# Division in the mixing stage of a decoder layer: logarithm, exponential and a Newton step in place of a reciprocal

## The chip, the cores and the metric

The kernel runs on one core of a Trainium2 chip. The metric is the device time of one execution, in microseconds (us), as the median of several runs. Engines are named as the profile names them: PE is TensorE, DVE is VectorE, ACT is ScalarE, POOL is GpSimd, SP issues DMAs.

## The reference, cut to what matters

The layer is an RWKV mixing, a cross attention, and a causal attention with a mixture of experts, each with a residual and a layer norm, on 16 x 128 tokens of 256 channels. Only the mixing is touched. For every channel it runs this scan over the 128 tokens of each batch, once forward and once backward:

```
ku = k_t + u
m = jnp.maximum(mx, ku)
e1 = jnp.exp(mx - m)
e2 = jnp.exp(ku - m)
y = (e1 * num + e2 * v_t) / (e1 * den + e2)
...
out_f = jax.nn.sigmoid(r_f) * wkv(k_f, v_f, -jnp.exp(time_decay), time_first, False)
```

The sigmoid's denominator, 1 + exp(-r), and the scan's denominator are multiplied together, so that there is one division for each element of the result: y = num / ((1 + exp(-r)) * den).

## The kernel before, in words

Seven stages run one after the other: preparing weights, mixing, cross attention, attention, routing, experts, finish. Each engine has its own instruction stream, written out by hand in program order, and semaphores tie the streams together. There is no scheduler: what stands behind a waiting instruction on its engine waits too.

The mixing cuts the work into 4 groups (`g`) of 4 batches = 512 token columns, and each group into 4 units (`u`): direction x half of the channels. So there are 16 units, n = 0 to 15, each on tiles of 128 channels x 512 tokens in f32. `in_groups` writes the first and the last group out and loops over the two between. For unit n:

- PE projects r, k and v into three PSUM banks (L519).
- ACT, `begin`: exp(-r) into `gate` (L565), v out of PSUM into `values` (L567), then, when DVE's `gaps` are there, two Relu and one Exp over `weight` (L570, L572, L574).
- DVE, `gaps`: the running maximum of the keys (L642, four scans that read PSUM) and two differences (L650, L652, one operand in PSUM).
- POOL, `new_parts`: two products of 128x512 (L596, L598). DVE, `scans`: two scans of 128x512 over SBUF tiles (L658, L661), for denominator and numerator. POOL, `add_old`: two products and two sums of 128x512 (L607 twice, L610, L611), which leave the denominator in `sums[p][:, 1]` and the numerator in `sums[p][:, 0]`.
- DVE, `finish`: (gate + 1) * denominator (L668), its reciprocal (L671), times the numerator into `y` (L675).
- PE adds y's projection to rows in PSUM (L534). At u = 2 DVE takes the previous group's layer norm statistics from them (`norm`, L681 to L689), POOL raises them to the power -1/2 (L615), and at u = 3 DVE scales the rows (`norm_rows`, L695).

The streams are staggered. In DVE's step n stand scans(n), gaps(n+2), at u = 3 norm_rows, then finish(n-1), and at u = 2 norm. In ACT's step n stands begin(n+2). In POOL's step n stand new_parts(n+1) and add_old(n). `gate` and `weight` have a buffer for each of the 4 units, `sums`, `values`, `new_value`, `carry` and `top` two each.

Of the kernel before, what the change touches and what calls it, by code (L numbers as in the profile page):

```python
# [32 lines left out]
UNITS = 4  # L33
# [14 lines left out]
BANKS_JOB = 4  # L48
MAGIC = 12582912.0
LOWEST = -1e38  # L50
MASKED = -1e30
EPS = 1e-5

# [42 lines left out]
class Shared:  # L96


    def __init__(self, nc, t, out, top):
# [17 lines left out]
        self.magic = self.buffer(top, "magic", [1])  # L117
        self.minus_magic = self.buffer(top, "minus_magic", [1])
        self.minus_half = self.buffer(top, "minus_half", [4])
        self.logits = self.buffer(top, "logits", [B, E])  # L120
        self.ident16 = self.buffer(top, "ident16", [P], BF16)
        self.shares = self.buffer(top, "shares", [2, B])
# [48 lines left out]
    def begin(self, sp, stage):  # L171

        sp.sem_inc(self.begun, 1)
# [249 lines left out]
def mix_stage(k):  # L423
# [31 lines left out]
    scans_ready = k.semaphore("scans_ready")  # L455
    sums_ready = k.semaphore("sums_ready")
    unit_done = k.semaphore("unit_done")
    unit_joined = k.semaphore("unit_joined")
    mix_var = k.semaphore("mix_var")
    mix_scale = k.semaphore("mix_scale")  # L460
# [96 lines left out]
    def scalar(act):  # L557
        st = k.steps["act"]

        def begin(u, n):  # L560

            p = u % 2
            act.wait_ge(rkv_ready, n + 1)
            act.wait_ge(unit_done, n + 1)
            act.activation(gate[u][:, :], banks[:, 3 * p, :], ACT.Exp, scale=-1.0)  # L565
            act.wait_ge(new_ready, 2 * n + 2)
            act.copy(values[p][:, :], banks[:, 3 * p + 2, :]).then_inc(vr_ready, 1)  # L567
            act.wait_ge(gaps_ready, n + 1)
            w = weight[u]
            st.did(act.activation(w[:, INNER, :], w[:, EDGES, :], ACT.Relu))  # L570
            st.wait()
            st.did(act.activation(w[:, EDGES, :], w[:, EDGES, :], ACT.Relu, scale=-1.0))  # L572
            st.wait()
            act.activation(w[:, :, :], w[:, :, :], ACT.Exp, scale=-1.0).then_inc(weights_ready, 1)  # L574

        def step(u, n, g, is_first, is_last):
            if u < 2 or not is_last:
                begin((u + 2) % UNITS, n + 2)

        act.wait_ge(k.begun, k.begins["mix"])  # L580
        act.wait_ge(k.mix_loads, 16 * LOADS)
        act.activation(step_decay[:, :], decay[:, :], ACT.Exp).then_inc(decay_ready, 1)
        begin(0, 0)
        begin(1, 1)
        st.done(1, 4)
        in_groups(step, act, st, 2 * UNITS)
        st.done(1, st.at)

    def gpsimd(pool):
# [43 lines left out]
    def vector(dve):  # L633
# [21 lines left out]
        def scans(u, n):  # L655
# [5 lines left out]
            dve.tensor_tensor_scan(carry[p][:, 0, 1:GT + 1], weight[u][:, FROM_PAST, :], new_value[p][:, 0, :],  # L661
                                   0.0, ALU.mult, ALU.add).then_inc(scans_ready, 1)

        def finish(u, n):

            p = u % 2
            dve.wait_ge(sums_ready, n + 5)
            st.did(dve.scalar_tensor_tensor(out=gate[u][:, :], in0=gate[u][:, :], scalar=1.0, in1=sums[p][:, 1, :],  # L668
                                            op0=ALU.add, op1=ALU.mult))
            st.wait()  # L670
            st.did(dve.reciprocal(sums[p][:, 1, :], gate[u][:, :]))  # L671
            st.wait()
            num, rec = (sums[p][:, m, :].rearrange("p (b s) -> p b s", b=GB) for m in range(2))
            to = y[:, u, :, :] if u < DC else y[:, u, :, ::-1]
            dve.tensor_tensor(to, num, rec, ALU.mult).then_inc(unit_done, 1)  # L675

        def norm(g):
            dve.wait_ge(unit_joined, UNITS * g + UNITS)
# [19 lines left out]

        def step(u, n, g, is_first, is_last):
            scans(u, n)  # L700
            if u < 2 or not is_last:
                gaps((u + 2) % UNITS, n + 2)
            if u == 3 and not is_first:
                norm_rows(g - 1)
            if u and not is_first:
                dve.wait_ge(unit_joined, n - UNITS)
            if u or not is_first:
                finish((u - 1) % UNITS, n - 1)
            if u == 2 and not is_first:
                norm(g - 1)  # L710
# [13 lines left out]
        gaps(1, 1)  # L724
        st.done(1, st.at)
        in_groups(step, dve, st, 3 * UNITS + 2)
        finish(UNITS - 1, N - 1)
        norm(GROUPS - 1)
        norm_rows(GROUPS - 1)
# [1522 lines left out]
def decoder_layer(nc, t, out):  # L2252
    with ExitStack() as top:
# [18 lines left out]
        @block.vector  # L2272
        def _(dve):
            k.steps["dve"] = Steps(dve, steps["dve"])
            dve.memset(k.magic[:, :], MAGIC).then_inc(k.s_fill, 1)
            dve.memset(k.minus_magic[:, :], -MAGIC).then_inc(k.s_fill, 1)
            dve.memset(k.minus_half[:, :], -0.5).then_inc(k.s_fill, 1)
            dve.wait_ge(k.s_consts, 16)
            for _, _, vector, *_ in stages:
                vector(dve)  # L2280

        @block.scalar
        def _(act):
            k.steps["act"] = Steps(act, steps["act"])
            act.wait_ge(k.s_consts, 16)
            act.wait_ge(k.s_fill, 3)
            for _, _, _, scalar, _ in stages:
                scalar(act)

        @block.gpsimd  # L2290
        def _(pool):
            k.steps["pool"] = Steps(pool, steps["pool"])
            pool.wait_ge(k.s_consts, 16)
            pool.wait_ge(k.s_fill, 3)
            for _, _, _, _, gpsimd in stages:
                gpsimd(pool)

# [75 lines left out]
```

## Time and profile before

| | |
|---|---|
| median of 3 runs | 1294.68 us (1290.55 to 1294.69) |
| the profiled execution's own time | 1292.86 us |
| its span in the trace | 1291.1 us |
| busy over the whole span | PE 78%, DVE 78%, ACT 57%, POOL 47% |
| mixing stage in the trace | from about 128 to 332 us |
| ACT_TABLE_LOAD | 2 in the whole kernel |

The shares are means over seven stages with different limits. The mixing stage is about a sixth of the span, and its own shares are in the rows further down.

### The profile page before, as it was taken

To read this page: it belongs to the slowest core of one execution; us is meant where nothing else is said; L and a number is where in the kernel's file an instruction comes from. 1 tells how busy PE (TensorE), PEld (TensorE's weight loads), DVE (VectorE), ACT (ScalarE), POOL (GpSimd) and SP (SyncE) were. 2 spreads that over 40 slices of the span, in tenths; PEclk is the share of its full clock that TensorE was granted. 3 is DMA by queue.
4 is the path that set the end of the run, shared out by engine and by line. 5 is a ranking of instruction groups with operands and counts; after the bars stand their busy time and mean duration, and the time that the engine had idled before them with its cause. 6 is when DMAs were issued, how large, how long until landed. Compare 5 with 4: busy or idle time off the path is not lost.

```text
span 1291.1 us, 25737 instructions
## 1 busy us (share of the span) xinstructions
PE 1005.1 (78%) x7366; PEld 756.9 (59%) x7367; DVE 1004.6 (78%) x2283; ACT 738.8 (57%) x1866; POOL 608.9 (47%) x805
## 2 busy tenths in 40 slices
PE   0334886772588898896799999983799999999980
PEld 0233332341477776774467767653688888888870
DVE  6894899999789888983788888856577777767755
ACT  4785644341488888882465555540566666666650
POOL 3896787776244444441255555543232332332225
PEclk9666978985789888986899999996899999999995
DMA  4953200002233333322123222230111111111105
GB/s 182 399 199 117 92 1 22 11 32 76 84 112 110 110 110 110 110 75 65 33 69 103 85 85 85 82 112 7 36 36 37 41 35 37 41 36 35 41 28 195
DMA packets 51884, 105.70 MB, mean 82 GB/s; under 512 B 9808, under 2 KB 36432, under 8 KB 51328
## 3 DMA queue, kind: packets, MB, share of 16 engines
q1 hardware_dynamic: 47472, 92.39, 20.8%
q0 software_dynamic: 4368, 12.78, 3.2%
q8 instruction: 20, 0.33, 0.1%
q14 instruction: 24, 0.20, 0.0%
HBM read 73.06 MB, written 32.10 MB: 81 GB/s over the span
## 4 chain that ended last, share of the span: by engine, by line
PE 48%; DVE 21%; issue 10%; POOL 6%; ACT 4%; DMA 1%; DVEq 0%; POOLq 0%; SPq 0%; ACTq 0%
PE banks L1996 14%; PE banks L2006 10%; PE banks L1360 4%; PE banks L1403 4%; DVE mix_sums L671 4%; PE banks L1382 2%; PE banks L1395 2%; POOL whole L1119 2%; PE banks L1352 2%; DVE carry L661 2%; ACT whole_level L1047 2%; DVE carry L658 2%; DVE whole_stat L227 2%; DVE peak L1150 1%; DVE top L642 1%
## 5 line engine op out<-in xcount | busy, mean ns | idle before, releaser
L2079 DVE SCALAR_TENSOR_TENSOR expert_gate<-banks,expert_steps,expert_chunk 128x128 f32<-128x128 f32 x546 | 166.1, 346 | 97.1 <-ACT expert_chunk L2041 92.7
L1996 PE MATMUL banks<-expert_parts,levels 128*128 128x128 bf16 x3276 | 228.8, 220 | 8.5 <-issue 5.6
L1996 PEld LDWEIGHTS banks<-expert_parts,levels 128*128 x3276 | 202.7, 98 | 49.2 <-issue 21.5
L2006 PE MATMUL banks<-down,up 128*128 x546 | 176.1, 406 | 0.0
L2041 ACT COPY expert_chunk<-banks 128x256 f32<-128x256 f32 x273 | 101.7, 372 | 102.4 <-PE banks L1996 87.9
L2134 POOL DMA_INDIRECT chosen_d<-expert_y,expert_target x39 | 39.1, 1001 | 203.5 <-ACT expert_y L2051 203.5
L519 PE MATMUL banks<-x_turned,w_rkv 128*128 128x512 f32 (+1 forms) x192 | 98.1, 670 | 38.8 <-DVE weight L652 38.3
L2045 ACT ACTIVATE silu<-expert_gate,expert_steps 128x128 f32<-128x128 f32 x273 | 110.7, 405 | 16.9 <-DVE expert_gate L2079 16.7
L414 PE MATMUL banks<-consts,level 128*128 128x128 f32 x154 | 35.6, 423 | 87.8 <-POOL level L397 87.8
L1119 POOL TENSOR_TENSOR whole<-whole_level,whole_stat 128x896 bf16<-128x896 f32 x32 | 53.3, 1686 | 102.4 <-DVE whole_level L1188 102.4
L2086 DVE SCALAR_TENSOR_TENSOR up<-expert_gate,expert_steps,silu 128x128 f32<-128x128 f32 x273 | 94.0, 344 | 9.3 <-ACT silu L2045 9.3
L519 PEld LDWEIGHTS banks<-x_turned,w_rkv 128*128 128x128 f32 x192 | 40.5, 217 | 94.1 <-issue 93.1
L1047 ACT ACTIVATE whole_level<-whole_raw,whole_stat 128x128 f32<-128x128 f32 x224 | 91.2, 485 | 6.9 <-DVE whole_stat L244 6.9
L414 PEld LDWEIGHTS banks<-consts,level 128*128 128x128 f32 x154 | 31.3, 226 | 91.3 <-POOL level L397 44.0
L2006 PEld LDWEIGHTS banks<-down,up 128*128 128x128 f32 x546 | 83.0, 191 | 0.4
L364 ACT ACTIVATE level<-raw,magic,stat 128x128 f32<-128x128 f32 x154 | 60.3, 480 | 20.0 <-DVE stat L263 20.0
L942 PE MATMUL banks<-v_ones,probs_t 128*128 128x17 f32 x512 | 63.7, 267 | 0.0
L1575 POOL TENSOR_TENSOR att_probs<-att_probs,att_share 128x1024 f32<-128x1024 f32 x16 | 30.4, 1897 | 70.2 <-DVE att_share L1692 70.2
L942 PEld LDWEIGHTS banks<-v_ones,probs_t 128*128 128x128 f32 x512 | 62.3, 199 | 0.0
L920 PE MATMUL banks<-spread,q_t 64*128 64x512 f32 x128 | 44.1, 768 | 23.2 <-DVE probs L1153 22.3
L1360 PE MATMUL banks<-attend_w,xn_t 128*128 128x512 f32 x128 | 59.0, 604 | 0.0
L1403 PE MATMUL banks<-attend_w,o_turn 128*128 128x256 f32 x256 | 58.1, 380 | 0.5 <-ACT logits L1506 0.5
(237 smaller groups left out, 2512.7 us busy)
## 6 DMA issues: line engine op xcount, KB each, us to landing
whole_raw<-in_weight_jobs SPq DMA_DIRECT2D x16, 896.0 KB, 5.3
raw<-in_weight_jobs SPq DMA_DIRECT2D x11, 896.0 KB, 5.4
numbers_d<-turned SPq DMA_DIRECT2D x11, 896.0 KB, 5.0
levels_d<-whole_t SPq DMA_DIRECT2D x16, 448.0 KB, 2.7
levels<-levels_d SPq DMA_DIRECT2D x16, 448.0 KB, 3.8
down<-numbers_d SPq DMA_DIRECT2D x16, 448.0 KB, 4.4
finish_moe<-chosen_d SPq DMA_DIRECT2D x8, 512.0 KB, 7.5
normed_d<-normed_parts SPq DMA_DIRECT2D x16, 192.0 KB, 1.9
```

The source lines that it names most:

```text
L519: last = pe.matmul(banks[:, 3 * (u % 2) + m, :], w_rkv[:, kc, col:col + P], x_turned[d][:, kc, bass.ds(g * GT, GT)], start=(kc == 0), stop ...
L942: last = pe.matmul(banks[:, HEADS, head * (XK + 1):(head + 1) * (XK + 1)], probs_t[h][:, 4 * m + a, :], v_ones[j][:, head, :], start=True, ...
L1047: last = act.activation(level[j][:, a, :], raw[j][:, a, :], ACT.Identity, bias=stat[j][:, BIAS, a:a + 1], scale=stat[j][:, INV, a:a + 1])
L1119: last = pool.tensor_tensor(whole[j][:, half, :], level[j][:, half, :], wide(stat[j][:, BIAS, half], P), ALU.subtract)
L1360: last = pe.matmul(banks[:, Q + m, :], xn_t[:, c, :], w_qkv[:, c, 512 * m:512 * m + 512], start=(c == 0), stop=(c == DC - 1))
L1403: last = pe.matmul(banks[:, TURN, 0:D], o_turn[:, h, :], w_o[:, h, :], start=(h == 0), stop=(h == QH - 1))
L1996: last = pe.matmul(banks[:, at, (m * DC + c) * ROWS:(m * DC + c + 1) * ROWS], levels[:, bass.ds(expert * (2 * JOB) + (m * JOB + (f * DC + ...
L2006: last = pe.matmul(banks[:, Y + j, 0:D], up[j][:, f, :], down[:, bass.ds(expert * JOB + f * D, D)], start=(f == 0), stop=(f == FC - 1))
L2041: act.copy(chunk[slot(j, f)][:, :, :], halves(at)[:, :, 0, :]).then_inc(chunk_ready, 1)
L2045: act.activation(silu[slot(j, f)][:, :], gate[slot(j, f)][:, 0, :], ACT.Silu, scale=steps[j][:, 0, 0, f:f + 1]).then_inc(silu_ready, 1)
L2079: last = dve.scalar_tensor_tensor(out=gate[slot(j, f)][:, m, :], in0=halves(at)[:, m, 1, :], scalar=steps[j][:, m, 1, f:f + 1], in1=chunk[ ...
L2086: dve.scalar_tensor_tensor(out=up[j][:, f, :], in0=gate[slot(j, f)][:, 1, :], scalar=steps[j][:, 1, 0, f:f + 1], in1=silu[slot(j, f)][:, : ...
```

## The change

`finish` is cut in two. DVE's `product(n-1)` multiplies gate and denominator; it now stands right behind scans(n), ahead of gaps(n+2), and waits for POOL's sums of unit n-1 and for `gates_ready`. The 1 + is taken out of it: ACT adds the one in `begin` (an Identity with a bias tile `ones`), and the product caps the gate at 1e30 instead. ACT's new `invert(n-1)` takes the logarithm of the product and then exp(-that). DVE's `finish(n-1)`, where it stood, makes one Newton step of two operations and the product with the numerator. ACT's former `begin` is split, so that its step is begin(n+2), invert(n-1), weigh(n+2). Three semaphores and one 128x1 buffer are new, with its fill at the kernel's start.

```diff
             act.wait_ge(unit_done, n + 1)
-            act.activation(gate[u][:, :], banks[:, 3 * p, :], ACT.Exp, scale=-1.0)
+            st.did(act.activation(gate[u][:, :], banks[:, 3 * p, :], ACT.Exp, scale=-1.0))
             act.wait_ge(new_ready, 2 * n + 2)
             act.copy(values[p][:, :], banks[:, 3 * p + 2, :]).then_inc(vr_ready, 1)
+            st.wait()
+            act.activation(gate[u][:, :], gate[u][:, :], ACT.Identity, bias=k.ones[:, 0:1]).then_inc(gates_ready, 1)
+
+        def weigh(u, n):
+
             act.wait_ge(gaps_ready, n + 1)
...
+        def invert(u, n):
+
+            p = u % 2
+            act.wait_ge(product_ready, n + 1)
+            st.did(act.activation(sums[p][:, 1, :], gate[u][:, :], ACT.Ln))
+            st.wait()
+            act.activation(sums[p][:, 1, :], sums[p][:, 1, :], ACT.Exp, scale=-1.0).then_inc(inverse_ready, 1)
+
         def step(u, n, g, is_first, is_last):
             if u < 2 or not is_last:
                 begin((u + 2) % UNITS, n + 2)
+            if u or not is_first:
+                invert((u - 1) % UNITS, n - 1)
+            if u < 2 or not is_last:
+                weigh((u + 2) % UNITS, n + 2)
...
-        def finish(u, n):
+        def product(u, n):
 
             p = u % 2
             dve.wait_ge(sums_ready, n + 5)
-            st.did(dve.scalar_tensor_tensor(out=gate[u][:, :], in0=gate[u][:, :], scalar=1.0, in1=sums[p][:, 1, :],
-                                            op0=ALU.add, op1=ALU.mult))
-            st.wait()
-            st.did(dve.reciprocal(sums[p][:, 1, :], gate[u][:, :]))
+            dve.wait_ge(gates_ready, n + 1)
+            dve.scalar_tensor_tensor(out=gate[u][:, :], in0=gate[u][:, :], scalar=LARGEST, in1=sums[p][:, 1, :],
+                                     op0=ALU.min, op1=ALU.mult).then_inc(product_ready, 1)
+
+        def finish(u, n):
+
+            p = u % 2
+            dve.wait_ge(inverse_ready, n + 1)
+            st.did(dve.tensor_tensor(gate[u][:, :], gate[u][:, :], sums[p][:, 1, :], ALU.mult))
+            st.wait()
+            st.did(dve.scalar_tensor_tensor(out=sums[p][:, 1, :], in0=gate[u][:, :], scalar=2.0, in1=sums[p][:, 1, :],
+                                            op0=ALU.subtract, op1=ALU.mult))
             st.wait()
             num, rec = (sums[p][:, m, :].rearrange("p (b s) -> p b s", b=GB) for m in range(2))
             to = y[:, u, :, :] if u < DC else y[:, u, :, ::-1]
-            dve.tensor_tensor(to, num, rec, ALU.mult).then_inc(unit_done, 1)
+            dve.scalar_tensor_tensor(out=to, in0=num, scalar=-1.0, in1=rec, op0=ALU.mult, op1=ALU.mult).then_inc(unit_done, 1)
...
             scans(u, n)
+            if u or not is_first:
+                product((u - 1) % UNITS, n - 1)
             if u < 2 or not is_last:
                 gaps((u + 2) % UNITS, n + 2)
```

DVE's stream in the kernel before, one step of the mixing loop (u = 1). In these listings the program's scans read as SCALAR_TENSOR_TENSOR with `carry` (`scans`) or `top` (`gaps`) as output.

```order
L658 SCALAR_TENSOR_TENSOR carry<-weight 128x512 [waits weights_ready]
L660 ISA
L661 SCALAR_TENSOR_TENSOR carry<-weight,new_value 128x512 [waits new_ready]
L642 SCALAR_TENSOR_TENSOR top<-step_decay,banks 128x128 [waits rkv_ready]
L642 SCALAR_TENSOR_TENSOR top<-step_decay,banks 128x128 x3
L72 REGISTER_ALU
L650 SCALAR_TENSOR_TENSOR weight<-top,step_decay,banks 128x512 [waits sums_ready,dve_steps]
L652 SCALAR_TENSOR_TENSOR weight<-banks,first,top 128x512
...
L668 SCALAR_TENSOR_TENSOR gate<-gate,mix_sums 128x512 [waits sums_ready]
L72 REGISTER_ALU
L671 RECIPROCAL mix_sums<-gate 128x512 [waits dve_steps]
L72 REGISTER_ALU
L675 TENSOR_TENSOR y<-mix_sums 128x512 [waits dve_steps]
```

The same step of the changed kernel:

```order
L682 SCALAR_TENSOR_TENSOR carry<-weight 128x512 [waits weights_ready]
L684 ISA
L685 SCALAR_TENSOR_TENSOR carry<-weight,new_value 128x512 [waits new_ready]
...
L693 SCALAR_TENSOR_TENSOR gate<-gate,mix_sums 128x512 [waits gates_ready,sums_ready]
L666 SCALAR_TENSOR_TENSOR top<-step_decay,banks 128x128 [waits rkv_ready]
...
L674 SCALAR_TENSOR_TENSOR weight<-top,step_decay,banks 128x512 [waits sums_ready,dve_steps]
L676 SCALAR_TENSOR_TENSOR weight<-banks,first,top 128x512
...
L700 TENSOR_TENSOR gate<-gate,mix_sums 128x512 [waits inverse_ready,unit_joined]
...
L702 SCALAR_TENSOR_TENSOR mix_sums<-gate,mix_sums 128x512 [waits dve_steps]
...
L707 SCALAR_TENSOR_TENSOR y<-mix_sums 128x512 [waits dve_steps]
```

The product of gate and denominator moved from behind the gaps to ahead of them, the reciprocal is gone, and two more operations on SBUF tiles stand in its place.

ACT's stream in the kernel before, one step of the first group:

```order
L565 ACTIVATE gate<-banks 128x512 [waits unit_done,rkv_ready]
L567 COPY values<-banks 128x512 [waits new_ready]
L570 ACTIVATE weight<-weight 128x1024 [waits gaps_ready]
L572 ACTIVATE weight<-weight 128x2x512 [waits act_steps]
L574 ACTIVATE weight<-weight 128x2048 [waits act_steps]
```

The same step of the changed kernel:

```order
L570 ACTIVATE gate<-banks 128x512 [waits unit_done,rkv_ready]
L572 COPY values<-banks 128x512 [waits new_ready]
L574 ACTIVATE gate<-gate,ones 128x512 [waits act_steps]
L590 ACT_TABLE_LOAD
L590 ACTIVATE mix_sums<-gate 128x512 [waits product_ready]
L592 ACT_TABLE_LOAD
L592 ACTIVATE mix_sums<-mix_sums 128x512 [waits act_steps]
L580 ACTIVATE weight<-weight 128x1024 [waits gaps_ready]
L582 ACTIVATE weight<-weight 128x2x512 [waits act_steps]
L584 ACTIVATE weight<-weight 128x2048 [waits act_steps]
```

The Identity, the logarithm and the exponential are new, and the build puts a table load ahead of each of the last two, in every step; the first load stands ahead of the wait for the product, the second behind the logarithm.

## Rows read from the trace of the kernel before

**Rows 1.** Busy time by stretch: the mixing stage; us, then PE, PEld, DVE, ACT, POOL, clock

```profile
128.00:332.00 204.00, 132.36 (x327) 67.36 (x326) 193.77 (x228) 81.23 (x80) 146.48 (x100) 0.84 0.12 42
```

**Rows 2.** Timeline, DVE, step of unit 9; start us, us, engine, line

```profile
239.15 0.69 DVE L675 TENSOR_TENSOR y<-mix_sums 128x512 f32<-128x512 f32 x1
239.75 2.29 DVE L658 TENSOR_TENSOR_SCAN carry<-weight 128x512 f32<-128x512 f32 x1
241.97 2.22 DVE L661 TENSOR_TENSOR_SCAN carry<-weight,new_value 128x512 f32<-128x512 f32 x1
244.11 1.32 DVE L642 TENSOR_TENSOR_SCAN top<-step_decay,banks 128x128 f32<-128x128 f32 x4
...
246.80 0.68 DVE L668 SCALAR_TENSOR_TENSOR gate<-gate,mix_sums 128x512 f32<-128x512 f32 x1
247.51 3.35 DVE L671 RECIPROCAL mix_sums<-gate 128x512 f32<-128x512 f32 x1
250.90 0.69 DVE L675 TENSOR_TENSOR y<-mix_sums 128x512 f32<-128x512 f32 x1
251.51 2.29 DVE L658 TENSOR_TENSOR_SCAN carry<-weight 128x512 f32<-128x512 f32 x1
```

**Rows 3.** Timeline, POOL, the same step

```profile
239.41 1.56 POOL L596 TENSOR_TENSOR new_value<-weight,values 128x512 f32<-128x512 f32 x1 [1.31 <-ACT weight L574]
240.93 2.18 POOL L598 TENSOR_TENSOR new_value<-weight,values 128x512 f32<-128x512 f32 x1
244.40 2.31 POOL L607 TENSOR_TENSOR mix_sums<-weight,carry 128x512 f32<-128x512 f32 x2 [1.29 <-DVE carry L661]
246.79 1.82 POOL L610 TENSOR_TENSOR mix_sums<-mix_sums,weight 128x512 f32<-128x512 f32 x1
248.57 1.27 POOL L611 TENSOR_TENSOR mix_sums<-mix_sums,new_value 128x512 f32<-128x512 f32 x1
```

**Rows 4.** Timeline, DVE, later steps: units 12 and 13, 14, 15, end of the stage

```profile
277.00 2.29 DVE L658 TENSOR_TENSOR_SCAN carry<-weight 128x512 f32<-128x512 f32 x1
...
287.72 2.29 DVE L658 TENSOR_TENSOR_SCAN carry<-weight 128x512 f32<-128x512 f32 x1
...
299.47 2.28 DVE L658 TENSOR_TENSOR_SCAN carry<-weight 128x512 f32<-128x512 f32 x1
...
310.57 1.22 DVE L658 TENSOR_TENSOR_SCAN carry<-weight 128x512 f32<-128x512 f32 x1
311.70 1.20 DVE L661 TENSOR_TENSOR_SCAN carry<-weight,new_value 128x512 f32<-128x512 f32 x1
...
320.00 0.68 DVE L668 SCALAR_TENSOR_TENSOR gate<-gate,mix_sums 128x512 f32<-128x512 f32 x1
...
324.11 0.69 DVE L675 TENSOR_TENSOR y<-mix_sums 128x512 f32<-128x512 f32 x1
```

**Rows 5.** Timeline, DVE, the stage's first steps: units 0, 1 and 4

```profile
150.71 0.69 DVE L668 SCALAR_TENSOR_TENSOR gate<-gate,mix_sums 128x512 f32<-128x512 f32 x1 [0.81 <-POOL mix_sums L611]
...
162.32 1.64 DVE L668 SCALAR_TENSOR_TENSOR gate<-gate,mix_sums 128x512 f32<-128x512 f32 x1
...
181.13 2.28 DVE L658 TENSOR_TENSOR_SCAN carry<-weight 128x512 f32<-128x512 f32 x1
```

**Rows 6.** Timeline, ACT, the step of rows 2

```profile
239.93 0.60 ACT L565 ACTIVATE gate<-banks 128x512 f32<-128x512 f32 x1 [0.68 <-DVE y L675]
240.42 0.58 ACT L567 COPY values<-banks 128x512 f32<-128x512 f32 x1
246.91 1.06 ACT L570 ACTIVATE weight<-weight 128x1024 f32<-128x1024 f32 x1 [5.91 <-DVE weight L652]
...
249.09 1.91 ACT L574 ACTIVATE weight<-weight 128x2048 f32<-128x2048 f32 x1
```

**Rows 7.** Timeline, ACT, the table load in the experts stage

```profile
913.40 0.37 ACT L2041 COPY expert_chunk<-banks 128x256 f32<-128x256 f32 x1 [0.85 <-PE banks L1996]
913.79 1.28 ACT L2045 ACT_TABLE_LOAD   x1
915.08 0.40 ACT L2045 ACTIVATE silu<-expert_gate,expert_steps 128x128 f32<-128x128 f32 x1
```

More of the change, by code:

```diff
@@ L50 @@
 LOWEST = -1e38
+LARGEST = 1e30
 MASKED = -1e30
@@ L119, in __init__ @@
         self.minus_half = self.buffer(top, "minus_half", [4])
+        self.ones = self.buffer(top, "ones", [1])
         self.logits = self.buffer(top, "logits", [B, E])
@@ L457, in mix_stage @@
     unit_done = k.semaphore("unit_done")
+    product_ready = k.semaphore("product_ready")
+    inverse_ready = k.semaphore("inverse_ready")
+    gates_ready = k.semaphore("gates_ready")
     unit_joined = k.semaphore("unit_joined")
@@ L582, in scalar @@
         act.activation(step_decay[:, :], decay[:, :], ACT.Exp).then_inc(decay_ready, 1)
[L583 to L586, printed above, removed]
+        for n in range(2):
+            begin(n, n)
+            weigh(n, n)
+        st.done(1, st.at)
+        in_groups(step, act, st, 4 * UNITS)
+        invert(UNITS - 1, N - 1)
         st.done(1, st.at)
@@ L662, in scans @@
                                    0.0, ALU.mult, ALU.add).then_inc(scans_ready, 1)
+        def product(u, n):
+            p = u % 2
+            dve.wait_ge(sums_ready, n + 5)
+            dve.wait_ge(gates_ready, n + 1)
+            dve.scalar_tensor_tensor(out=gate[u][:, :], in0=gate[u][:, :], scalar=LARGEST, in1=sums[p][:, 1, :],
+                                     op0=ALU.min, op1=ALU.mult).then_inc(product_ready, 1)
         def finish(u, n):
             p = u % 2
-            dve.wait_ge(sums_ready, n + 5)
-            st.did(dve.scalar_tensor_tensor(out=gate[u][:, :], in0=gate[u][:, :], scalar=1.0, in1=sums[p][:, 1, :],
-                                            op0=ALU.add, op1=ALU.mult))
+            dve.wait_ge(inverse_ready, n + 1)
+            st.did(dve.tensor_tensor(gate[u][:, :], gate[u][:, :], sums[p][:, 1, :], ALU.mult))
             st.wait()
-            st.did(dve.reciprocal(sums[p][:, 1, :], gate[u][:, :]))
+            st.did(dve.scalar_tensor_tensor(out=sums[p][:, 1, :], in0=gate[u][:, :], scalar=2.0, in1=sums[p][:, 1, :],
+                                            op0=ALU.subtract, op1=ALU.mult))
             st.wait()
@@ L726, in vector @@
         in_groups(step, dve, st, 3 * UNITS + 2)
+        product(UNITS - 1, N - 1)
         finish(UNITS - 1, N - 1)
@@ L2277, in _ @@
             dve.memset(k.minus_half[:, :], -0.5).then_inc(k.s_fill, 1)
+            dve.memset(k.ones[:, :], 1.0).then_inc(k.s_fill, 1)
             dve.wait_ge(k.s_consts, 16)
@@ L2285, in _ @@
             act.wait_ge(k.s_consts, 16)
-            act.wait_ge(k.s_fill, 3)
+            act.wait_ge(k.s_fill, 4)
             for _, _, _, scalar, _ in stages:
@@ L2293, in _ @@
             pool.wait_ge(k.s_consts, 16)
-            pool.wait_ge(k.s_fill, 3)
+            pool.wait_ge(k.s_fill, 4)
             for _, _, _, _, gpsimd in stages:
```

## The prediction

> **What bounds the kernel now.** I read the mixing stage by itself, since nothing else is touched: the busy time by stretch first, then the timelines of DVE, POOL and ACT side by side over one step, then the stage's two ends. In the stage DVE is busy 193.8 of 204 us, POOL 146.5, ACT 81.2 [rows 1]. DVE has no idle time in a steady step: from one L658 to the next is 251.51 - 239.75 = 11.76 us [rows 2], namely scans 4.36 (239.75 to 244.11), gaps 2.69 (to 246.80), L668 0.71, reciprocal 3.39, L675 0.61. The step is as long as DVE's stream. What the reader is to see next is that the scans are not as long as they could be. Where POOL is not at the same work, one follows the other after 1.13 us (310.57 to 311.70) [rows 4]; in the steady step they take 2.2 each, while POOL's L596 and L598, which take 1.27 like L611 when alone, last 1.56 and 2.18 [rows 3]. Laid side by side the four go one after another: L675 ends at 239.84, and from there to 244.11 are 4.27 us for two scans (2 x 1.07) and two POOL operations (2 x 1.07). So a POOL operation and a DVE operation with two SBUF operands exclude each other, and whoever waited goes next. It also holds for short ones: POOL's L610 beside L668 has 1.82 instead of 1.27, 0.55 longer, and L668 itself, 0.68 when alone, has 1.64 where POOL held first [rows 3, 5]. The reciprocal reads one operand and lies beside L610 and L611 at no cost to L611. So the reciprocal's 3.39 us are also a stretch in which POOL has the way free.
>
> The Trainium skill says the same in "SBUF — State Buffer", section on the ports of SBUF: VectorE and GpSimd share a port pair, a VectorE operation with two SBUF inputs takes it, and it is held for the whole instruction while the other blocks. The trace agrees in kind (0.55 us longer); if each were to hold for its full record (1.27 and 0.69 rather than 1.1 and 0.55), the step worked out below would be 12.0 instead of 11.5 us.
>
> **The change, part by part.** DVE, per unit: the reciprocal goes, -3.39. L668 stays as the product, 0.66. Two operations come, each 0.71 with its wait, as L668 to L671 in [rows 2]. Without any contention DVE's step would be scans 2.26, product 0.66, gaps 2.69, three finishing operations 0.71 + 0.71 + 0.61: 7.6 us. With the contention of before on the scans (4.36 instead of 2.26) it is 9.7, 2.0 less than now.
>
> ACT, per unit: exp and copy 1.07 (239.93 to 241.00) and the three on `weight` 4.09 (246.91 to 251.00) stay [rows 6]. New are Identity, Ln and Exp of 128x512, for which I take L565's 0.60 each, and two table loads of 1.28 [rows 7]. Sum 1.07 + 4.09 + 1.8 + 2.56 = 9.5 us. In [rows 7] the load starts 0.02 us behind the end of the copy ahead of it (913.77), and the next activation starts 0.01 behind its end, so a load is 1.3 us here and nothing more. The first load stands ahead of the wait and is hidden in ACT's idle time, the second is in the chain: from the product's end to the inverse there are Ln 0.6, load 1.28, Exp 0.6 and hand-overs, 2.65 us. The gaps behind the product take 2.69 us on DVE, so this is just covered where there are gaps. If that cover is gone (units 13 to 15, no gaps left) it is exposed.
>
> What is late next is the shared way to SBUF. Per step POOL has six operations there and DVE had four (two scans, L668, L675); now DVE has six. In lock time: POOL 6 x 1.1 = 6.6, scans 2.1, and 0.55 for each short one: before 2 x 0.55, sum 9.8; after 4 x 0.55, sum 10.9 of a step of 11.76. I lay a steady step out, from the first scan at 0. The weights for the next unit come at about 0.3, so L596 falls between the scans: scan 1.1, L596 2.2, scan 3.3, L598 4.4, product 4.95, its next instruction 5.07. POOL's two L607 then run beside the gaps, 4.95 to 7.35 with their 2.39 to the next operation (244.40 to 246.79 [rows 3]), L610 to 8.5. Gaps end at 7.76, and the inverse is ready at 7.7, but the first Newton operation waits for L610: 8.5 to 9.05. L611 waited and takes 9.05 to 10.15, the second Newton operation waits for it until 10.7, the last one runs 10.85 to 11.4, next scan 11.45. So the two added short operations cost not 1.4 but 1.4 plus two waits of about 1 us, and the step is **11.5 against 11.76**. ACT's weights are ready at 7.76 + 4.09 = 11.85, that is 0.4 into the next step, which closes the circle; ACT has 2 us to spare.
>
> With norm at u = 2 the step has 2.07 more, as before. At u = 3 POOL is held by L615 until the scans are through, and its L596 then stands against the product: 11.6. At u = 0 the step was 10.72 (277.00 to 287.72 [rows 4]), since POOL's L596 was ahead by then; that advantage goes, because POOL's last operation of the step before is now late: 11.5. A group is 11.5 + 13.5 + 11.6 + 11.5 = 48.1, against 299.47 - 251.51 = 47.96 [rows 2, 4]. From unit 4 to unit 14 that makes +0.9 us; if POOL's operation counts 1.22 rather than 1.1 (L610 and L611 stand 1.78 apart with one L668 between them), the same layout gives 11.9 and +3.1. I take +1.5, nearer the first, since the four that surely exclude each other gave 1.07.
>
> The start: the product now stands ahead of gaps(3) and waits for POOL's first sums, which came at 150.7 with DVE already waiting 0.81 behind the gaps [rows 5]. gaps(3), 2.69 us, now lie behind that wait, and so do the weights of unit 3. Laid out in the same way, unit 4's scan comes at 183.4 instead of 181.13: +2.3 (bounds: 0 if POOL's backlog hides it, 4 for gaps and the inverse exposed once).
>
> The last group: at unit 14 no gaps cover the inverse. Product at 4.95, inverse at 7.7, against L610 and L611, then norm: 13.5 against 310.57 - 299.47 = 11.1: +2.4. Unit 15: norm_rows (1.8) covers part of the inverse and POOL has no L596 and L598: 9.4 against 320.00 - 310.57 = 9.43: 0. The tail: L668 at 320.00 to the end of L675 at 324.80 is 4.8; after it is 0.66 + 2.65 + 0.71 + 0.71 + 0.69 = 5.4: +0.6.
>
> Sum: 2.3 + 1.5 + 2.4 + 0 + 0.6 = **+6.8 us**. The bias tile and its fill at the start lie beside the first loads. ACT's Identity delays the first weights by 0.6, which is in the start's term. PE has 132 of 204 us in the stage and is two units ahead; its clock there is 0.84 of full speed. The stages behind start when the mixed rows are stored, so the stage's end moves theirs one for one. Against the profiled execution (time 1292.86, span 1291.1) this is 1299.7. The median of the runs is 1.8 above the profiled one, so I say 1300.
>
> **Rivals.**
>
> A. The way to SBUF is full and takes back what the reciprocal gives, as above: +2 to +10 us, 1296 to 1304. For it: scans and L596/L598 in a strict row [rows 2, 3]. Against: the order in which the waiting ones go is seen there on long operations only. Chance 0.72.
>
> B. Faster: the short operations slip between POOL's, because POOL waits at its own hand-overs (c. 0.1 us each) and DVE wins. Then the step falls towards DVE's 9.7 or ACT's 9.5. At 9.7 it is 12 steps x 2.0 = -24, plus 5 for both ends: 1274; at 10.9, the lock time alone, 12 x 0.85 = -10, plus 5: 1288. For it: L668 at 246.80 got through although POOL's L610 started at 246.79. It decides from a gain of 0.5 us a step on, where the ends are paid for. Chance 0.16.
>
> C. Slower by far: ACT becomes the bound. It has 9.5 of 11.5 us; from 1 us more for each load on it does. The Trainium skill, "ScalarE: Activation LUTs", section on what a table load costs, gives about 1283 ns and a further drain of about 1380 ns for each switch of set; the row agrees with the first and has nothing of the second. If a load did cost twice its own 1.28, ACT's step would be 9.5 + 2.6 = 12.1 against A's 11.5, and the chain from product to inverse 1.3 longer at three places without cover: 12 x 0.6 + 3 x 1.3 = 11 on top of A's 6.8, 1311. Chance 0.12.
>
> **How the numbers follow.** The likeliest is A at 1300. About 0.5% (6.5 us) is what this kernel's measurement tells from no change: faster is below 1288.2, slower above 1301.2. A puts 0.40 of its chance within and 0.30 above, with 0.02 below; B gives 0.12 faster and 0.04 within; C gives 0.11 slower and 0.01 within. Faster 0.14, same 0.45, slower 0.41. The range 1287 to 1307 holds A, the upper part of B and the lower part of C, and leaves out some 0.2. A's own range is 1296 to 1304.
>
> **What would show it.** In the changed profile: the first Newton operation (L700) and the second (L702) have records of well over 0.7 us, about 1.3 to 1.7, at most units; L707 about 0.7. No reciprocal in the mixing. 32 table loads of 1.28 us, the next activation right behind each. ACT busy about 81 + 16 x 4.4 = 151 us of the stage. POOL's L611-like operation about 1.3 to 1.8. DVE busy about as before, though its work alone is less. Steps of 11.3 to 12 us. DVE's idle time ahead of L700 is small, but for the last three units (2.7 us each at most). The prediction is wrong if L700 and L702 are 0.7 each and the step is under 11 us, or if DVE waits for ACT in steady steps.

## The result and the profile after

The changed kernel takes 1295.47 us (median of 20 runs, 1292.72 to 1298.44), the kernel before 1291.61 us (median of 20, 1286.06 to 1295.42). The ratio is 1.0029, 95% interval 1.0015 to 1.0042: 3.7 us slower by the ratio, and clearly so, though less than 0.5%. The mixing stage, from the first scan to the end of the last `y`, was 187.62 us (137.18 to 324.80) and is 192.10 us (139.02 to 331.12) in the profiled execution of each kernel: +4.5 us.

Timeline of the changed kernel, DVE in one steady step (unit 5); the columns are start us, us, engine, line, operation, and in brackets the idle time before with what ended it:

```profile
196.07 1.22 DVE L682 TENSOR_TENSOR_SCAN carry<-weight 128x512 f32<-128x512 f32 x1
197.20 2.24 DVE L685 TENSOR_TENSOR_SCAN carry<-weight,new_value 128x512 f32<-128x512 f32 x1
199.36 1.69 DVE L693 SCALAR_TENSOR_TENSOR gate<-gate,mix_sums 128x512 f32<-128x512 f32 x1
200.97 1.34 DVE L666 TENSOR_TENSOR_SCAN top<-step_decay,banks 128x128 f32<-128x128 f32 x4
...
204.12 1.01 DVE L700 TENSOR_TENSOR gate<-gate,mix_sums 128x512 f32<-128x512 f32 x1 [0.36 <-issue]
205.16 1.64 DVE L702 SCALAR_TENSOR_TENSOR mix_sums<-gate,mix_sums 128x512 f32<-128x512 f32 x1
206.83 0.69 DVE L707 SCALAR_TENSOR_TENSOR y<-mix_sums 128x512 f32<-128x512 f32 x1
207.44 1.22 DVE L682 TENSOR_TENSOR_SCAN carry<-weight 128x512 f32<-128x512 f32 x1
```

POOL in the same step, with L620 and L622 for `new_parts`, L631, L634 and L635 for `add_old`:

```profile
196.66 1.69 POOL L620 TENSOR_TENSOR new_value<-weight,values 128x512 f32<-128x512 f32 x1 [1.78 <-ACT weight L584]
198.32 2.17 POOL L622 TENSOR_TENSOR new_value<-weight,values 128x512 f32<-128x512 f32 x1
200.46 2.76 POOL L631 TENSOR_TENSOR mix_sums<-weight,carry 128x512 f32<-128x512 f32 x2
203.30 1.27 POOL L634 TENSOR_TENSOR mix_sums<-mix_sums,weight 128x512 f32<-128x512 f32 x1
204.53 1.72 POOL L635 TENSOR_TENSOR mix_sums<-mix_sums,new_value 128x512 f32<-128x512 f32 x1
```

ACT in the same step, from the first table load to the last Exp over `weight`:

```profile
198.10 1.28 ACT L590 ACT_TABLE_LOAD   x1
201.08 0.63 ACT L590 ACTIVATE mix_sums<-gate 128x512 f32<-128x512 f32 x1 [1.70 <-DVE gate L693]
201.73 1.28 ACT L592 ACT_TABLE_LOAD   x1
203.02 0.63 ACT L592 ACTIVATE mix_sums<-mix_sums 128x512 f32<-128x512 f32 x1
203.79 1.06 ACT L580 ACTIVATE weight<-weight 128x1024 f32<-128x1024 f32 x1
...
205.97 1.92 ACT L584 ACTIVATE weight<-weight 128x2048 f32<-128x2048 f32 x1
```

What to see: the step is 207.44 - 196.07 = 11.37 us, against 11.76 in [rows 2]. The reciprocal's 3.39 us are gone, and the product's record has grown from 0.68 to 1.69, the second Newton operation takes 1.64 and the first 1.01, each behind an operation of POOL: L700 behind L634, L702 behind L635, L693 behind L622. Ahead of L700 DVE has the only idle time of the step, 0.36. ACT waits 1.70 for the product, so it has time to spare at that place. POOL's own idle time, 1.78 ahead of L620, ends with the weights of ACT's L584, which follow the gaps by 4.1 us (203.76 to 207.89); no run shortens these three operations, so how much of the step hangs on this circle from the gaps over ACT's weights to POOL is not shown. Where POOL is through, the same three operations take 0.69 each, as at the very end of the stage, where the chain through ACT lies open instead (timeline of the changed kernel, DVE, units 13 and 15):

```profile
306.24 1.68 DVE L693 SCALAR_TENSOR_TENSOR gate<-gate,mix_sums 128x512 f32<-128x512 f32 x1
310.63 1.35 DVE L700 TENSOR_TENSOR gate<-gate,mix_sums 128x512 f32<-128x512 f32 x1 [2.71 <-ACT mix_sums L592]
312.02 1.63 DVE L702 SCALAR_TENSOR_TENSOR mix_sums<-gate,mix_sums 128x512 f32<-128x512 f32 x1
313.69 0.69 DVE L707 SCALAR_TENSOR_TENSOR y<-mix_sums 128x512 f32<-128x512 f32 x1
...
325.65 0.69 DVE L693 SCALAR_TENSOR_TENSOR gate<-gate,mix_sums 128x512 f32<-128x512 f32 x1
328.97 0.69 DVE L700 TENSOR_TENSOR gate<-gate,mix_sums 128x512 f32<-128x512 f32 x1 [2.64 <-ACT mix_sums L592]
329.70 0.69 DVE L702 SCALAR_TENSOR_TENSOR mix_sums<-gate,mix_sums 128x512 f32<-128x512 f32 x1
330.43 0.69 DVE L707 SCALAR_TENSOR_TENSOR y<-mix_sums 128x512 f32<-128x512 f32 x1
```

Piece by piece, from first scan to first scan: units 0 to 4, 43.95 before and 45.68 after (+1.7); units 4 to 14, 118.34 and 118.27 (-0.1); unit 14, 11.10 and 13.39 (+2.3); from unit 15's scan to the end, 14.23 and 14.76 (+0.5).

Busy time by stretch of the changed kernel, the row that answers to [rows 1]:

```profile
128.00:332.00 204.00, 135.24 (x327) 68.06 (x326) 185.21 (x231) 151.22 (x160) 151.81 (x99) 0.84 0.12 42
```

ACT went from 81 to 151 us, POOL from 146 to 152 (its work is the same, but waits for the shared way lie inside the records and count as busy), DVE from 194 to 185. ACT and POOL are now each busy for about three quarters of the stretch, and the stage is no shorter.

The two profiled spans differ by 1.8 us only (1291.1 and 1292.9), although the stage ends 6.3 us later. Of these 6.3 us, 1.8 arose before the first scan. PE's first projections began 0.7 us earlier than before (123.16 against 123.86), but the granted clock was 0.50 and 0.61 in the two stretches from 123 to 129 us, where the kernel before had 0.96 and 1.00, and they ended later. This is not the new division's doing: e1, which has none of it, had 0.50 and 0.71 there and its first scan at 139.02 too, and e5, which has it, had 1.00 and its first scan at 136.79. And 3.5 us went the other way at the end of the cross stage, which nothing of the change touches: the projections of its last row stand 5.75 us later than before, those of the attention behind it 2.23. There PE ran the same last pieces at other levels of its clock. Busy time by stretch, kernel before, 585 to 600 us; PE stands first, its clock is the number after POOL's:

```profile
585.00:600.00 15.00, 12.02 (x61) 10.34 (x60) 2.95 (x9) 4.63 (x8) 2.00 (x2) 0.58 0.20 64
```

The same of the changed kernel, 588 to 602 us:

```profile
588.00:602.00 14.00, 12.20 (x76) 9.56 (x74) 5.72 (x11) 6.77 (x13) 3.88 (x3) 0.78 0.29 96
```

In both kernels PE had been almost without a pause at full clock just before (granted clock 1.00; 13.1 of 14 us and 10.3 of 11 us busy), then fell to the lower of its two levels (1.2 of 2.4 GHz), and in the changed kernel came back sooner. By these two shifts, 1.8 us one way and 3.5 the other, two single spans can differ by some 2 to 4 us in which the change has no part (an estimate from this one pair). The stage's own length and the many runs are what the experiments are read by.

### The profile page after: what moved, and what is told of

Read it like the earlier page. It is cut to its first block, busy times and chain, and to the rows that moved or that the text cites. A ratio compares the mean times of both kernels' runs of the same rounds, so it can differ in the third digit from the quotient of the medians.

```text
span 1292.9 us, 25876 instructions
## 1 busy us (share of the span) xinstructions
PE 1007.1 (78%) x7366; PEld 756.4 (59%) x7367; DVE 999.7 (77%) x2300; ACT 808.5 (63%) x1946; POOL 614.0 (47%) x805
## 4 chain that ended last, share of the span: by engine, by line
PE 47%; DVE 22%; issue 11%; POOL 7%; ACT 3%; DMA 1%; DVEq 0%; POOLq 0%; SPq 0%; ACTq 0%
PE banks L2031 14%; PE banks L2041 10%; PE banks L1395 4%; PE banks L1438 4%; PE banks L1417 2%; PE banks L1430 2%; POOL whole L1154 2%; DVE whole_stat L229 2%; PE banks L1387 2%; DVE carry L685 2%; DVE mix_sums L702 2%; DVE peak L1185 2%; DVE gate L693 1%; DVE gate L700 1%; DVE top L666 1%
## 5 line engine op out<-in xcount | busy, mean ns | idle before, releaser
L524 PE MATMUL banks<-x_turned,w_rkv 128*128 128x512 f32 (+1 forms) x192 | 102.0, 692 | 40.4 <-DVE weight L676 39.9
L977 PEld LDWEIGHTS banks<-v_ones,probs_t 128*128 128x128 f32 x512 | 59.7, 192 | 0.2 <-ACT probs_t L1067 0.2
```

The source lines that it names most:

```text
L524: last = pe.matmul(banks[:, 3 * (u % 2) + m, :], w_rkv[:, kc, col:col + P], x_turned[d][:, kc, bass.ds(g * GT, GT)], start=(kc == 0), stop ...
L977: last = pe.matmul(banks[:, HEADS, head * (XK + 1):(head + 1) * (XK + 1)], probs_t[h][:, 4 * m + a, :], v_ones[j][:, head, :], start=True, ...
```

## The experiments

The theories. **S**: DVE and POOL share a way to SBUF, one operation at a time; the reciprocal was a stretch in which POOL had it free, and the two added operations on it take back what the reciprocal gave. **L**: the two table loads and the chain through ScalarE take it back. **M**: the move of the product ahead of the gaps does. "Stage" is always first scan to end of the last `y`.

**e1_moved_only.** The kernel before with the move alone:

```diff
-        def finish(u, n):
+        def product(u, n):
...
                                             op0=ALU.add, op1=ALU.mult))
+
+        def finish(u, n):
+
+            p = u % 2
             st.wait()
...
             scans(u, n)
+            if u or not is_first:
+                product((u - 1) % UNITS, n - 1)
```

> The kernel before with the product of gate and denominator moved ahead of the gaps, and nothing else; the reciprocal stays. Theory S (the way to SBUF that DVE and POOL share takes back what the reciprocal gives): the move itself costs only at the start, where gaps(3) come to stand behind POOL's first sums: unit 4's first scan 1.5 to 2.5 us later after unit 0's than in the kernel before, steady steps 11.7 to 11.9 (DVE's own work is unchanged, the product now meets POOL's L598-like operation but the steady step loses the meeting with L610), whole kernel +1 to +3 us. Theory M (the move to the front of the gaps is what costs in every step): steady steps of 12.3 or more, +8 us or more.

Measured: ratio to before 1.0021 (1.0002 to 1.0040), 2.7 us; stage 190.68, +3.1. Units 0 to 4 take 45.07 (+1.1), steady steps 11.57. The start was over-sized and the steady step with 11.7 to 11.9 as well, the total is as S has it and far from M's 8 us. The step at u = 3 went from 11.65 to 12.6, though, and units 4 to 14 cost 1.6. So with the reciprocal in place the move alone costs 3.1 us of stage, as much as two thirds of what the whole change costs, and by the ratios (2.7 and 3.7 us, with intervals that overlap) the two can't be told apart. That these 3.1 us are contained in the 4.5 is not shown, since in the changed kernel the same move saves time (e10). What the move does not explain is why the new division, which without more contention was to take 2.0 us off a step, takes off 0.2 (11.57 to 11.36).

**e2_loads_gone.** The changed kernel with a Relu of tiny scale for the logarithm, so that no table is loaded in the mixing; the quotient is not computed:

```diff
-            st.did(act.activation(sums[p][:, 1, :], gate[u][:, :], ACT.Ln))
+            st.did(act.activation(sums[p][:, 1, :], gate[u][:, :], ACT.Relu, scale=1e-31))
```

> The changed kernel with the logarithm replaced by a Relu with a tiny scale, so that the same number of ScalarE operations of the same size stand in the chain but no table is loaded in the mixing (the quotient is not computed). Theory S: steady steps stay at 11.36 (the chain from product to inverse is covered by gaps and by the wait for POOL), ACT busy 41 us less, the gain is 1.3 us at each place where L700 waited for the inverse (three): whole kernel 2 to 4 us faster than the changed kernel, ratio to before 0.999 to 1.001. Theory L (the table loads are what takes back the gain): steady steps fall to 10.1 or less, 15 us or more faster than the changed kernel.

Measured: ratio 1.0012 (0.9992 to 1.0031), 2.2 us below the changed kernel's ratio, with intervals that overlap. The stage tells it better: 190.13, 2.0 less than after, all of it from unit 14 on, where the chain through ACT lies open; units 4 to 14 take 118.38 against 118.27. 41 us of ScalarE's time are gone, and the steady steps do not move. So the loads are not what takes the gain back; the rest of L, the chain through ScalarE, is tried in e10.

**e3_small_sums_before** and **e4_small_sums_after.** The kernel before and the changed kernel, both with POOL's last two operations of a unit cut to 4 of 512 columns, which leaves out the adding of the new part, and with the two products ahead of them turned into sums of the same size:

```diff
-                last = pool.tensor_tensor(sums[p][:, m, :], weight[u][:, OLD, :], carry[p][:, m, 0:GT], ALU.mult)
+                last = pool.tensor_tensor(sums[p][:, m, :], weight[u][:, OLD, :], carry[p][:, m, 0:GT], ALU.add)
...
-            pool.tensor_tensor(sums[p][:, 1, :], sums[p][:, 1, :], weight[u][:, NOW, :], ALU.add)
-            pool.tensor_tensor(sums[p][:, 0, :], sums[p][:, 0, :], new_value[p][:, 1, :], ALU.add).then_inc(sums_ready, 1)
+            pool.tensor_tensor(sums[p][:, 1, 0:4], sums[p][:, 1, 0:4], weight[u][:, NOW, 0:4], ALU.add)
+            pool.tensor_tensor(sums[p][:, 0, 0:4], sums[p][:, 0, 0:4], new_value[p][:, 1, 0:4], ALU.add).then_inc(sums_ready, 1)
```

> The kernel before with POOL's two sums of add_old (L610, L611) cut to 4 of 512 columns and its products turned into sums so that denominators stay above zero: what is left out is the adding of the new part. Theory S: these two lie beside the reciprocal, which leaves the way free, so almost nothing is gained: steady step 11.6 to 11.8, whole kernel -3 to +0.5 us (the first steps, where DVE waited for POOL's sums, gain up to 3). Theory L: the same.

> The changed kernel with the same cut of POOL's two sums. Theory S: the Newton operations no longer wait, so the step falls from 11.36 to 9.8 to 10.0, where ScalarE's 9.7 us of work take over; the whole kernel is 15 to 22 us faster than the changed kernel, and 12 to 20 us faster than the kernel before with the same cut: the change, a loss in the real kernel, becomes a clear gain. Theory L (loads and ScalarE's chain bound the step) and theory M: the step stays at 11 us or more and the pair differ by less than 5 us.

Measured: e3 0.9960 (0.9937 to 0.9983), stage 182.66; its steady step is 11.75, as before, and all it gains is in the start (39.01 for units 0 to 4, -4.9, more than the 3 expected). e4 0.9805 (0.9766 to 0.9843), stage 163.57, steps 9.3 to 9.9. Between the pair are 19.1 us of stage, 1.55% of the kernel, for the very change that costs 0.3% with the two sums whole. Against the changed kernel e4's stage is 28.5 us shorter, more than the 22 expected. Timeline of e4, DVE at the end of a step:

```profile
257.08 0.68 DVE L700 TENSOR_TENSOR gate<-gate,mix_sums 128x512 f32<-128x512 f32 x1
257.79 0.69 DVE L702 SCALAR_TENSOR_TENSOR mix_sums<-gate,mix_sums 128x512 f32<-128x512 f32 x1
258.51 0.69 DVE L707 SCALAR_TENSOR_TENSOR y<-mix_sums 128x512 f32<-128x512 f32 x1
```

POOL's two sums in the same step:

```profile
256.12 0.20 POOL L634 TENSOR_TENSOR mix_sums<-mix_sums,weight 128x4 f32<-128x4 f32 x1
256.27 0.20 POOL L635 TENSOR_TENSOR mix_sums<-mix_sums,new_value 128x4 f32<-128x4 f32 x1
```

The three finishing operations stand at 0.7 us from one to the next. This is the strongest of the runs: the loads, the chain through ScalarE and the move are all still in e4, and L and M had the pair within 5 us.

**e5_no_newton.** The changed kernel without the Newton step; the sign and DVE's count of its steps go with it, and nothing else is changed:

```diff
-            st.did(dve.tensor_tensor(gate[u][:, :], gate[u][:, :], sums[p][:, 1, :], ALU.mult))
-            st.wait()
-            st.did(dve.scalar_tensor_tensor(out=sums[p][:, 1, :], in0=gate[u][:, :], scalar=2.0, in1=sums[p][:, 1, :],
-                                            op0=ALU.subtract, op1=ALU.mult))
-            st.wait()
...
-            dve.scalar_tensor_tensor(out=to, in0=num, scalar=-1.0, in1=rec, op0=ALU.mult, op1=ALU.mult).then_inc(unit_done, 1)
+            dve.scalar_tensor_tensor(out=to, in0=num, scalar=1.0, in1=rec, op0=ALU.mult, op1=ALU.mult).then_inc(unit_done, 1)
```

> The changed kernel without the two Newton operations: the inverse from Ln and Exp is used as it is, so what is left out is its refinement. Theory S: two short operations and one wait for POOL (L634 or L635) leave DVE's stream, and the shared way has 9.8 instead of 10.9 us of work a step; but ScalarE's own 9.7 us and the inverse (ready at 7.7) then bound it: steady step 9.9 to 10.4 instead of 11.36, 13 to 19 us faster than the changed kernel. Rival (each Newton operation costs its own 0.7 us and no more): step 9.95 as well by counting 1.4 off; to be told apart by the records: by S the last product (L707's place) has 1.3 us or more and the next scan meets L635.

Measured: 1268.96 us, ratio 0.9830 (0.9802 to 0.9857), 22 us faster than the kernel before. The stage is 165.82, 26.3 less than after, where 13 to 19 was expected: the steady step is 10.1 as expected, and the start gains another 6.7 (38.94 for units 0 to 4). Timeline of e5, DVE:

```profile
236.51 1.24 DVE L702 SCALAR_TENSOR_TENSOR y<-mix_sums 128x512 f32<-128x512 f32 x1
237.68 2.29 DVE L682 TENSOR_TENSOR_SCAN carry<-weight 128x512 f32<-128x512 f32 x1
239.89 2.23 DVE L685 TENSOR_TENSOR_SCAN carry<-weight,new_value 128x512 f32<-128x512 f32 x1
```

POOL in the same step:

```profile
237.28 1.60 POOL L634 TENSOR_TENSOR mix_sums<-mix_sums,weight 128x512 f32<-128x512 f32 x1
238.85 2.19 POOL L635 TENSOR_TENSOR mix_sums<-mix_sums,new_value 128x512 f32<-128x512 f32 x1
241.12 2.06 POOL L620 TENSOR_TENSOR new_value<-weight,values 128x512 f32<-128x512 f32 x1
```

The last product has 1.24, just short of the 1.3 by which S was to be told from its rival, and the next scan meets L635, as S has it (2.29 where it takes 1.2 alone). With two short operations gone, POOL's L635 now stands between the scans.

**e6_pool_order_before** and **e7_pool_order_after.** POOL's two parts of a step swapped, in the kernel before and in the changed one:

```diff
+            add_old(u, n)
             if u < 3 or not is_last:
                 new_parts((u + 1) % UNITS, n + 1)
-            add_old(u, n)
```

> The kernel before with POOL's two parts of a step swapped: add_old(n) first, then new_parts(n+1). Then all six POOL operations fall beside gaps and reciprocal instead of L596 and L598 beside the scans. Theory S: the scans go back from 2.2 to 1.2 us each and the steady step falls from 11.76 to 10.3 to 10.9; whole kernel 8 to 18 us faster. If the scans were slow for another reason: no change.

> The changed kernel with the same swap of POOL's parts. Theory S: there is no stretch of 3.4 us left in which POOL has the way free, the sum on the shared way stays 10.9 us a step, so the step is 10.8 to 11.4 and the gain 0 to 6 us against the changed kernel; it ends 6 to 14 us slower than the swapped kernel before. Rival (the order on POOL is what cost, not the sum): both swapped kernels gain the same, and stay 4 us apart.

Measured: e6 1284.06 us, ratio 0.9945 (0.9925 to 0.9965), stage 180.37; e7 1291.18 us, 1.0003 (0.9988 to 1.0018), stage 187.94. e6's steady step is 10.75, within the forecast, though the whole gains 7 us and not 8 to 18: step 1 (14.39 against 11.96) and the end (15.82 against 14.23) lose some. e7's steady step is 11.34, unmoved. The pair differ by 7.5 us: in the steady step the swap pays only where a reciprocal leaves POOL a free stretch. It is worth something in the changed kernel too, though: e7's stage is 4.2 us shorter than the changed kernel's, 1.5 of it in units 0 to 4 and some 1.1 at each step with u = 3 (11.5 against 12.6), so that e7 is level with the kernel before. S had put this at 0 to 6 us. Timeline of e6, DVE:

```profile
244.12 3.35 DVE L671 RECIPROCAL mix_sums<-gate 128x512 f32<-128x512 f32 x1
247.51 0.72 DVE L675 TENSOR_TENSOR y<-mix_sums 128x512 f32<-128x512 f32 x1
248.15 2.28 DVE L658 TENSOR_TENSOR_SCAN carry<-weight 128x512 f32<-128x512 f32 x1
250.35 1.19 DVE L661 TENSOR_TENSOR_SCAN carry<-weight,new_value 128x512 f32<-128x512 f32 x1
```

POOL beside it:

```profile
243.40 1.81 POOL L610 TENSOR_TENSOR mix_sums<-mix_sums,weight 128x512 f32<-128x512 f32 x1
245.18 1.27 POOL L611 TENSOR_TENSOR mix_sums<-mix_sums,new_value 128x512 f32<-128x512 f32 x1
246.41 1.27 POOL L596 TENSOR_TENSOR new_value<-weight,values 128x512 f32<-128x512 f32 x1
247.63 1.72 POOL L598 TENSOR_TENSOR new_value<-weight,values 128x512 f32<-128x512 f32 x1
```

L611 and L596 run at 1.27 beside the reciprocal (244.12 to 247.47), where L596 and L598 had 1.56 and 2.18 [rows 3]; only L598 still meets a scan.

**e8_no_newton_lean** and **e9_lean_pool_order.** e5 with the one added by DVE in the product again, instead of by ScalarE, and the same with the swap of e6:

```diff
-            st.wait()
-            act.activation(gate[u][:, :], gate[u][:, :], ACT.Identity, bias=k.ones[:, 0:1]).then_inc(gates_ready, 1)
...
-            dve.wait_ge(gates_ready, n + 1)
-            dve.scalar_tensor_tensor(out=gate[u][:, :], in0=gate[u][:, :], scalar=LARGEST, in1=sums[p][:, 1, :],
-                                     op0=ALU.min, op1=ALU.mult).then_inc(product_ready, 1)
+            dve.wait_ge(vr_ready, n + 1)
+            dve.scalar_tensor_tensor(out=gate[u][:, :], in0=gate[u][:, :], scalar=1.0, in1=sums[p][:, 1, :],
+                                     op0=ALU.add, op1=ALU.mult).then_inc(product_ready, 1)
```

> The run without the Newton step, and besides the one of 1 + exp(-r) added again by DVE in the product (as in the kernel before) instead of by ScalarE's Identity; the cap at 1e30 falls away with it. In the run without Newton ScalarE had no idle time left ahead of anything but 0.25 us and the step was 10.1. Theory S: ScalarE's work falls by 0.6 us to 9.4 a step, and the shared way (six operations of POOL, four of DVE, 9.8 us) takes over: steady step 9.7 to 10.0, 2 to 6 us faster than without Newton alone. Rival (ScalarE was not the bound there): step stays 10.1, no gain.

> The same, with POOL's two parts swapped as in the swapped kernel before. Theory S: without a long one-operand stretch on DVE the swap moves the meetings but not their sum: step 9.7 to 10.3, within 4 us of the lean kernel either way. If POOL's order counted by itself: 5 us or more faster.

Measured: e8 0.9859 (0.9832 to 0.9886), stage 165.10, steady step 10.1, the same as e5's; ACT, relieved, just waits longer for the product (timeline of e8, ACT, the logarithm):

```profile
243.09 0.63 ACT L588 ACTIVATE mix_sums<-gate 128x512 f32<-128x512 f32 x1 [0.88 <-DVE gate L691]
```

0.88 us, against 0.25 at the same place in e5. So the rival was right here: ScalarE did not bound e5, although it had almost no idle time left. What did is seen in the steady steps of both. POOL has no idle time there: in e5 one L634 starts at 186.96 and the next at 197.07, 10.11 us for six operations that take 1.27 each or some 7.5 together when nothing blocks them, and DVE waits for POOL's sum (timeline of e5, DVE):

```profile
191.21 0.69 DVE L693 SCALAR_TENSOR_TENSOR gate<-gate,mix_sums 128x512 f32<-128x512 f32 x1 [1.09 <-POOL mix_sums L635]
```

The bound is POOL's stream, made longer by its waits for DVE's operations on the shared way. e9 0.9871 (0.9844 to 0.9899), stage 167.87, step 10.25: the swap buys nothing here, as expected.

**e10_product_in_place.** The changed kernel with the product back behind the gaps:

```diff
             scans(u, n)
-            if u or not is_first:
-                product((u - 1) % UNITS, n - 1)
...
             if u or not is_first:
+                product((u - 1) % UNITS, n - 1)
                 finish((u - 1) % UNITS, n - 1)
```

> The changed kernel with the product of gate and denominator back behind the gaps, directly ahead of the Newton operations, so that the chain from product to inverse (2.65 us) is not covered by gaps. Theory S: DVE waits some 2.6 us for the inverse in each step, but POOL uses that time, and its L634 and L635 no longer stand between the Newton operations: steady step 10.8 to 11.8, and the start does not wait for POOL's first sums (unit 0 to unit 4 at 44 us instead of 45.7); whole kernel within 4 us of the changed one. Theory L (the chain through ScalarE is what costs): the step is 12.4 or more, the sum of DVE's own work and the wait with the old contention, whole kernel 12 us or more slower.

Measured: 1301.10 us, ratio 1.0068 (1.0044 to 1.0092), stage 198.62, steady step 11.85. Timeline of e10, DVE:

```profile
240.08 1.48 DVE L693 SCALAR_TENSOR_TENSOR gate<-gate,mix_sums 128x512 f32<-128x512 f32 x1
244.20 1.44 DVE L700 TENSOR_TENSOR gate<-gate,mix_sums 128x512 f32<-128x512 f32 x1 [2.64 <-ACT mix_sums L592]
245.67 0.69 DVE L702 SCALAR_TENSOR_TENSOR mix_sums<-gate,mix_sums 128x512 f32<-128x512 f32 x1
246.39 0.69 DVE L707 SCALAR_TENSOR_TENSOR y<-mix_sums 128x512 f32<-128x512 f32 x1
247.00 1.22 DVE L682 TENSOR_TENSOR_SCAN carry<-weight 128x512 f32<-128x512 f32 x1
```

DVE stands idle 2.64 us for the inverse in every step, and yet the step is only 0.5 longer than the changed kernel's 11.36: POOL uses the time, L702 is back at 0.69 and both scans at 1.2. That is S's side of it, just past its upper end of 11.8; the whole is 5.0 us slower by the ratios than the changed kernel, a little over the 4 expected, and the start did not gain (46.77, not 44). The move ahead of the gaps is worth its price: with this division it saves 6.5 us of stage.

## Why the prediction was wrong in its class and right in its mechanism

- **What bounds the step: right.** The layout by hand had L700 behind POOL's L610 and L702 behind L611 (now L634 and L635), the step at 11.45. Measured 11.36, in that order.
- **Norm step, u = 3, u = 0: right in sum only.** Forecast 13.5, 11.6, 11.5; measured 13.4, 12.6, 10.4. The step that failed is "that advantage goes, because POOL's last operation of the step before is now late". It is not late: the last L635 ahead of the scans at 233.51 starts at 229.50 and takes 1.71, and POOL still runs ahead of the scans. The price is paid at u = 3, where L707 waits for L620 (timeline of the changed kernel, DVE at the end of unit 7's step):

```profile
231.79 1.79 DVE L707 SCALAR_TENSOR_TENSOR y<-mix_sums 128x512 f32<-128x512 f32 x1
233.51 2.28 DVE L682 TENSOR_TENSOR_SCAN carry<-weight 128x512 f32<-128x512 f32 x1
```

POOL beside it:

```profile
231.78 1.26 POOL L620 TENSOR_TENSOR new_value<-weight,values 128x512 f32<-128x512 f32 x1 [0.57 <-ACT weight L584]
233.00 1.71 POOL L622 TENSOR_TENSOR new_value<-weight,values 128x512 f32<-128x512 f32 x1
```

- **The steady term of the sum: mis-sized.** For units 4 to 14 the layout said +0.9, I took +1.5 on account of a longer hold by POOL, measured -0.1. These 1.6 us are the largest part of the 2.3 by which the sum exceeds the stage's 4.5. The longer hold ("if POOL's operation counts 1.22 rather than 1.1") did not come either: L700, issued at 204.12, took 1.01 instead of 0.69, so L634, started at 203.30, kept it back until about 204.44, which is 1.14 us.
- **The start: right, over-sized.** +2.3 forecast, +1.7 measured, of which e1 gives 1.1 to the move. **The last group: right.** +2.4 for unit 14 against +2.3; 0 and +0.6 for the rest against +0.5 together. L700 waited 2.71 and 2.64 us for the inverse at units 13 and 15 and 0.9 at unit 14, where norm_rows covers part.
- **The table loads: right.** 32 loads in the mixing, each 1.283 us, and where the next activation had nothing else to wait for it stood 0.01 to 0.02 us behind. Rival C, with a load at twice its price, ScalarE's step at 12.1 us and the kernel at 1311, did not come. The Trainium skill, "ScalarE: Activation LUTs", section "What ACT_TABLE_LOAD costs", gives about 1283 ns and a further drain of about 1380 ns for each switch. The trace agrees with the first and shows no such drain at any load of the mixing.
- **Rival B: wrong.** The short operations do not slip through: in each steady step L634 goes ahead of L700 and L635 ahead of L702.
- **The sum: +6.8 forecast, +4.5 in the stage, +3.7 by the ratio.** 1300 lies 4.5 above the measured 1295.5: 2.9 are the sum's terms, the rest is the base, as I put the sum on a profiled run of 1292.86 and read the median of three runs as above it, while the median of twenty is 1291.61, below it.
- **The step that failed in the verdict** is in how the numbers follow: "About 0.5% (6.5 us) is what this kernel's measurement tells from no change". I had the direction and a sum above zero in every part, and made "no change" the likeliest class on the strength of that bound. The interval came out at a quarter of it, 0.14% either way, and 0.29% is outside it. A sum whose terms are all zero or above is a forecast of slower.

## What to carry to other kernels

An engine's stretch on one operand or on PSUM can be what lets its neighbour run, as the 3.35 us of reciprocal did here: before a long operation is replaced by several short ones, count the operations that both engines send to the shared way to SBUF, not only the busy time of the one that is relieved. The same change is worth -1.55% or +0.3% depending on two operations of another engine (e3 to e4). Of the kernels with full sums that were run, the new division pays only without its Newton step (e5, 22 us faster than the kernel before), where the bare inverse is precise enough. And where a reciprocal is to stay, move the other engine's work beside it (e6, 7 us faster than the kernel before).

## What the runs showed of the hardware

- Whoever waits for the shared way goes next: L634, L700, L635, L702 in the steady step. A blocked operation's wait is inside its record: in the changed kernel 128x512 in f32 with two SBUF operands has 0.69 alone and up to 1.79 blocked on DVE, 1.27 and up to 2.2 on POOL. POOL's hold is about 1.1 of the 1.27 us of its record (1.14 by L634 and L700). The Trainium skill, "SBUF — State Buffer", section "Who interferes with whom", says that a VectorE instruction with two SBUF inputs contends with a GpSimd instruction that reads SBUF. The traces agree.
- DVE's reciprocal of 128x512 takes 3.35 us and does not hold POOL up (L611 1.27 beside it).
- Ln behind Exp and Exp behind Ln each had a table load in this build. The Trainium skill, "ScalarE: Activation LUTs", section "Table sets: the hidden batching unit", names a set with both, for which one load would do. No run here shows that; e2, without any of these loads, bounds what it could bring here: 2.0 us of stage.
- A saturated engine need not be the bound: in e5 ScalarE waited 0.25 to 0.44 us a step, and taking 0.6 us of work from it changed nothing (e8).
